# Gathered rows of a graph convolution spread over the full spans only, instead of every third step

## The reference, cut to what matters

```python
def _gcn_conv(x, src, dst, dout, din, W, b):
    m = (x * dout[:, None])[src]
    agg = jax.ops.segment_sum(m, dst, num_segments=N)
    return agg * din[:, None] @ W + b
dout, din = _degree_norms(src, dst)
h = _gcn_conv(in_feat, src, dst, dout, din, W1, b1)
for _ in range(1, PROP_STEP):          # PROP_STEP = 2
    h = _gcn_conv(h, src, dst, dout, din, W2, b2)
```

## Time and profile before

| | |
|---|---|
| median of 3 runs | 7628.19 us (7626.54 to 7639.28) |
| the profiled execution, its own time | 7633.74 us |
| its span in the profile | 7631.9 us |
| busy share PE, PEld, DVE, ACT, POOL | 87%, 73%, 62%, 45%, 64% |
| gathers L1021 | 1408, mean 1107 ns, 1558.9 us busy |
| casts of counts L1174 | 1120, mean 585 ns |
| dense matmuls L1209 | 4480 + 3360, mean 393 and 388 ns |

### The profile page before, as it was taken

The page is one execution under the profiler, slowest core; times in us unless marked ns, Lnnn a source line. Parts: engine busy times, 40 slices in busy tenths (PEclk is TensorE's granted clock), DMA queues, the critical chain, the costliest instruction groups (busy, mean ns, idle before and its releaser), DMA issues.

```text
span 7631.9 us, 125666 instructions
## 1 busy us (share of the span) xinstructions
PE 6610.3 (87%) x37688; PEld 5557.3 (73%) x37689; DVE 4745.0 (62%) x9176; ACT 3399.5 (45%) x6948; POOL 4890.1 (64%) x4864
## 2 busy tenths in 40 slices
PE   6999978999987999986888888888888888888887
PEld 4666656888876888875777777777777777777776
DVE  9999984333334333337666666666666666666665
ACT  5999975555545555543223232222222222222222
POOL 2211104777764777764777777777777777777775
PEclk9999999999999999998777777877777777778777
DMA  3666556555545555545333333333333333333332
GB/s 81 133 130 131 124 121 192 164 167 165 169 126 167 167 168 166 167 131 141 84 85 85 84 84 85 84 84 85 84 87 84 84 85 84 85 84 84 85 84 55
DMA packets 604288, 868.27 MB, mean 114 GB/s; under 512 B 217476, under 2 KB 470459, under 8 KB 599025
## 3 DMA queue, kind: packets, MB, share of 16 engines
q0 software_dynamic: 158000, 437.63, 23.3%
q1 hardware_dynamic: 419980, 414.22, 19.3%
q10 hardware_dynamic: 26036, 12.80, 0.6%
HBM read 706.92 MB, written 157.30 MB: 113 GB/s over the span
## 4 chain that ended last, share of the span: by engine, by line
POOL 34%; issue 13%; DMA 3%; DVE 2%; POOLq 1%; DVEq 0%; PE 0%; SPq 0%; ACT 0%; ACTq 0%
POOL t_rows L1779 34%; DMA t_rows<-table,t_ends 2%; DMA t_attrs<-in_edge_attr 1%; DVE t_msg_ad L2043 1%; POOLq L179 0%; DVE t_msg_bc L2057 0%; DVE t_cg L2042 0%; SPq L1751 0%; DVE t_msg_ad L2045 0%; POOLq L1777 0%; DVE t_ge L2039 0%; PE t_sums L1958 0%; DVE t_rel L2130 0%; PE t_sums L1961 0%; DVE acc L2020 0%
## 5 line engine op out<-in xcount | busy, mean ns | idle before, releaser
L1779 POOL DMA_INDIRECT t_rows<-table,t_ends x3224 | 3047.4, 945 | 1005.9 <-issue 967.2
L1021 POOL DMA_INDIRECT c_early<-table,c_first_src x1408 | 1558.9, 1107 | 661.2 <-issue 453.6
L1800 ACT ACTIVATE t_weight<-t_weight,t_attrs 128x64 f32<-128x64 f32 x3224 | 692.0, 302 | 2095.4 <-PE t_weight L1901 2068.9
L1958 PEld LDWEIGHTS t_sums<-t_hot,t_msg_ad 128*128 128x128 f32 x6464 | 952.9, 232 | 922.6 <-issue 922.3
L1096 ACT ACTIVATE c_wide_act<-c_raw 128x1024 fp32r<-128x1024 uint8 (+1 forms) x1120 | 1160.1, 1039 | 881.2 <-PE c_sums L1209 877.6
L1958 PE MATMUL t_sums<-t_hot,t_msg_ad 128*128 x6464 | 987.5, 318 | 621.4 <-DVE t_hot L2137 620.3
L1174 DVE CAST c_wide_dve<-c_raw 128x1024 fp32r<-128x1024 uint8 (+1 forms) x1120 | 653.0, 585 | 1258.6 <-PE c_sums L1209 1257.3
L1209 PE MATMUL c_sums<-c_wide_act,c_parts 128*128 128x512 f32 (+1 forms) x4480 | 1211.5, 393 | 73.9 <-DVE c_parts L1158 63.5
L2039 DVE TENSOR_TENSOR t_ge<-t_rows,t_edge 128x768 f32<-128x768 f32 x403 | 384.3, 954 | 1201.5 <-DMA t_rows<-table,t_ends 1187.8
L1961 PE MATMUL t_sums<-t_hot,t_msg_bc 128*128 x6464 | 1089.1, 340 | 0.0
L1961 PEld LDWEIGHTS t_sums<-t_hot,t_msg_bc 128*128 128x128 f32 x6464 | 1053.2, 255 | 0.0
(11 more groups left out here) (240 smaller groups left out, 6744.6 us busy)
## 6 DMA issues: line engine op xcount, KB each, us to landing
c_raw<-a_dram SPq DMA_DIRECT2D x532, 448.0 KB, 3.5
a_dram<-a_a_sb POOLq DMA_DIRECT2D x39, 3136.0 KB, 18.2
t_scal<-in_edge_attr SPq DMA_DIRECT2D x403, 256.0 KB
t_rows<-table,t_ends POOLq DMA_INDIRECT x3224
c_early<-table,c_first_src POOLq DMA_INDIRECT x1408, 3.2
t_ends<-in_edges SPq DMA_DIRECT2D x403, 8.0 KB
t_attrs<-in_edge_attr SPq DMA_DIRECT2D x403, 16.0 KB
c_raw<-a_dram SPq DMA_DIRECT2D x28, 224.0 KB, 2.6
```

The costliest lines, as they stand in the source:

```text
L1021: pool.indirect_dma_start(out=rows_of_group[:, q % 2, t], out_offset=None, in_=table_of_rows, in_offset=bass.IndirectOffsetOnAxis(ap=c.fir ...
L1779: pool.indirect_dma_start(out=rows[:, slot, t, :], out_offset=None, in_=table, in_offset=bass.IndirectOffsetOnAxis(ap=ends[:, slot, t:t + ...
L1800: mul = act.activation(ad, ad, ACT.Copy, scale=attrs[:, slot, t, 0:1])
L1958: pe.matmul(sums[:, of, 0:WIDE], msg_ad[:, slot % 2, t, :], hot[:, of, t, :], start=t == 0, stop=t == T - 1)
```

## The change

The step of group q becomes 15 + floor(252 q / 88), written out in a table `after`; 252 is 18 spans of 14 steps. The gaps between groups are 2 or 3 steps (15, 17, 20, 23, 26, 29, 32, 35, 37, ..., 258, 261, 264). The last group belongs to step 264, and its sum ends step 265, the last one of full width. Nothing else differs.

```diff
-STEPS_OF_N = 3
...
         def group_after(n):
 
-            q, rest = divmod(n - NHC - 1, STEPS_OF_N)
-            return q if rest == 0 and 0 <= q < SG else None
+            return after.get(n)
 
         table_of_rows = table if scaled is None else scaled
-        assert NHC + 2 + (SG - 1) * STEPS_OF_N < NSPAN * NHC
+        after = {NHC + 1 + q * ((NSPAN - 2) * NHC) // SG: q for q in range(SG)}
+        assert len(after) == SG
```

## The result

The changed kernel took 7681.1 us in the median of six runs (7672.73 to 7685.74) beside 7633.72 us for the kernel before (7626.54 to 7642.02): a ratio of 1.0061, 95% interval 1.0048 to 1.0074, so 47 us slower. The forecast was slower, by 30 us, with a range that holds it. Its profiled execution has a span of 7673.7 us, 41.8 us over that of before, and lies at the low end of its runs.

What follows compares the result with a forecast made beforehand. GpSimd's gather issue was taken to bound the convolutions beside TensorE; terms of +15.3 and +15.0 us, +30 us together, gave 7664 us on the profiled time, 7658 on the median, stated as 7660 us, range 7615 to 7690.

Steps and rivals of the forecast that it cites:

- GpSimd sets when the last sum can start: Both convolutions: GpSimd's gather issue, 11.50 and 11.45 us a group, sets the time until the last group.
- the likeliest case: Whole kernel: the forecast itself, slower by 30 us at 7660 us, given 68%.
- The rival that the rows keep up: Both convolutions: GpSimd follows TensorE's 10.9 us a group, 51 us less together, 7579 us; chance 10%.
- The tail: After each convolution's last sum: 14 half-width steps left instead of two, +20.2 us.
- The holding by casts: GpSimd's gathers: held by six VectorE casts and one comparison, 1.58 us of 11.50 us a group.
- The comparison is a holder too, as chosen: VectorE's hot-matrix comparison: counted as holding gathers, so two-step groups save 2/7 of the holding, not 2/6.
- The two-step groups and the gains after waits: Twelve groups a convolution meet four casts, not six: -5.4 and -5.2 us; six TensorE waits delay casts: -3.9 us each convolution.
- the four moved groups: Groups 84 to 87, moved into a full span, are issued at its price: +3.2 and +2.7 us.
- From last gather to its sum: End of each convolution: 2.83 us in a full span, 1.63 us in the half span before: +1.2 us.
- the clock, which stood among the rivals: TensorE at half clock after each of twelve waits, not hidden: 20 us a convolution, 7698 us; chance 6%.

Runs made afterwards that it cites:

- the second profile: The changed kernel run and profiled once more, nothing altered: 7680.15 us, ratio 1.005 to the kernel before; its profiled execution took 7692.43 us.
- the kernel that ends at step 278: Changed kernel with the 88 groups spread to step 278 instead of 264, last sum after the last step: 7633.66 us, 0.9989 of the kernel before.

## Why the prediction was right, and where it was short

**GpSimd sets when the last sum can start**: right, and the likeliest case came. Nothing in the changed profile makes a gather wait for TensorE, and with half the gathers or with casts that don't hold them the loss is gone. The rival that the rows keep up needs groups under 11.2 us; they took 11.37 and 11.43. GpSimd isn't free of TensorE's pace, though: in the kernel before, the sums of groups 16 to 27 of the first convolution come 11.35 us apart, each 5.68 us after its last gather. GpSimd waits for no semaphore there, but the casts that hold its gathers go at TensorE's pace.

**The tail**, +20.2 us a convolution: 25.46 - 5.32 = 20.1 us measured, in both, and in both profiles.

**The holding by casts** as the cause of the gathers' pace was argued from single rows; the reduction form shows it: in the old placement the gathers' time beyond 0.94 us each falls from 119.0 and 116.3 us to 27.5 and 28.6. (The 1.58 us of holding a group was read too high: the durations give 1.35 us, and the rest is the late starts told at the end.) The comparison is a holder too, as chosen: with casts that don't hold, 106 of the 107 slow gathers meet it. The addition that follows it is not the holder: the five gathers that meet it alone take 0.94 us. The Trainium skill ("SBUF — State Buffer", Who interferes with whom) expects a two-input comparison not to stop descriptor writing and calls that inferred; in the same section such an instruction does contend with a GpSimd instruction that reads SBUF. Here gathers that begin inside it take 1.22 us in the mean of 119, those clear of it 0.94 us; which of GpSimd's accesses is held, no run here shows.

**What was mis-sized**: two terms, together the 17 us between 30 and 47.
*The two-step groups and the gains after waits*, with the four moved groups, were summed as -6.1 us and -6.4 us on the gathers' time (3.2 - 5.4 - 3.9 and 2.7 - 5.2 - 3.9). Measured, against before: -6.5 and +2.4 us in the first profile, +2.9 and +4.0 in the second, +0.7 in the mean. Gathers' time beyond 0.94 us each, all 88 groups, was 119.0 and 116.3 us before, 112.2 and 114.5 after, and 119.5 and 117.0 in the second profile. Taken apart, by the means: the four moved groups are held 3.5 us more, about as summed; the other 84 are held 5.4 us less and not some 9; and gathers that start late without being held (told at the end) add 2.6 us, for which the sum had no term. Profiles of like placement scatter by as much as these terms (113.9 and 120.8 us on those 84 groups in the kernel that ends at step 278). The count of casts does matter where two-step gaps lie in a row: in the kernel with all twelve at the end, the last twelve groups are held 0.56 and 0.72 us each, the other 76 groups 1.41 and 1.44. Single two-step gaps give back less.
*From last gather to its sum*, +1.2 us by 2.83 us where before had 1.64 and 2.08: 3.10, 6.98, 6.98 and 5.67 us. What was missing is the clock, which stood among the rivals. The timeline of TensorE in the changed kernel, at its first two-step gap:

```profile
1262.28 2.22 PE L1189 MATMUL c_few<-c_early 128*128 128x64 f32 x16 [2.98 <-DMA c_early<-table,c_first_src]
1264.26 2.05 PE L1208 MATMUL c_sums<-c_wide_act,c_parts 128*128 128x512 f32 x4
1275.33 0.89 PE L1189 MATMUL c_few<-c_early 128*128 128x64 f32 x7
```

After the wait of 2.98 us four matmuls take 2.05 us instead of the 1.07 of the earlier trace rows, and the next sum comes 13.05 us later instead of 11.35; elsewhere in this trace 14.6 us. The granted clock (the column before the last two), 1.00 in the full spans before, is 0.77 behind that wait (1265 to 1270), a mix of 1.2 and 2.4 GHz:

```profile
1265.00:1270.00 5.00, 5.00 (x19) 3.99 (x18) 1.98 (x4) 2.12 (x2) 3.78 (x5) 0.77 0.33 74
```

TensorE's sums then start up to 7 us after their last gather, 4 us after their rows, and keep that distance through gaps of three steps, since both engines go at 11.35 us there; a two-step gap takes up 3 us of it. Where the last groups follow such a wait, the convolution ends with TensorE late: at most 4 us, not the 20 us of that rival. The prediction took the wait's good side (the gathers gain) and not this one.

By the means of the two profiles, then, gathers +0.7 instead of -6.3 us and landing +3.8 instead of +1.2 us a convolution are some 10 us, or 19 us in both, and the tail came as summed. That accounts for the two profiled executions (the second on another chip), which lie 50 us in the mean over the one before, 20 more than forecast; the medians miss by 17. The prediction also gives 7579 us for the rows keeping up where its own terms make 7577, which changes nothing.

## What to carry to other kernels

When two engines share a pace, look which one never waits: it is the bound even where the other is nearly always busy, and work moved away from a late stall only moves the wait if the bound's own chain is untouched. What can run beside the bound's last items should stay beside them; a tail that depends on nothing is worth keeping as cover. If a gather is issued by GpSimd, ask first what VectorE runs during it: changing the form of a cast, slower by itself, was worth 29 us (7599.79 against 7629.27) and with the spread 41 us (7588.01); the best placement alone gave some 8 us.

## What was not expected of the hardware

A reduction over an axis of length one widens bytes to float32 without holding GpSimd's gathers: 0.94 us in the mean over the 1222 gathers clear of a comparison, at 932 ns a cast in place of 582.

In each convolution of each kernel with all gathers, the second gather of groups 14, 28, 42, 56, 70 and 84, counted from 0 and so every 112th, comes 2 to 4.5 us after the one before it instead of 0.30 (1.3 to 3.6 us with the casts as a reduction), put down to "issue". A row of the changed kernel:

```profile
2897.76 0.94 POOL L1020 DMA_INDIRECT c_early<-table,c_first_src  x1 [4.53 <-issue]
```

Beyond 0.30 us each, the six add up to 13.4 and 11.8 us before and 13.7 and 16.0 us after. With half of the gathers it is again every 112th gather, now the second of groups 28, 56 and 84, and there it waits 0.64 us. A row of the old placement:

```profile
1547.59 0.94 POOL L1021 DMA_INDIRECT c_early<-table,c_first_src  x1 [0.64 <-issue]
```

So it goes by the count of gathers and not by group or time, and is shorter where they come more slowly. What it waits for stays open.
